# A four-layer graph network on one core: a reordered setup, and one-input maxima for the first batch

## The chip, the core and the metric

The kernel runs on one core of one Trainium2 chip. Time is device time of one execution in microseconds; lower is better. The engines are TensorE (PE, with its weight loads PEld), VectorE (DVE), ScalarE (ACT), GpSimd (POOL) and SyncE (SP); "ACTq" and "SPq" are DMAs that ScalarE's and SyncE's instruction streams issue.

## The reference, cut to what matters

Eight graphs (batches) of 2048 nodes with 256 features, one adjacency matrix of 0 and 1 each. Four layers, each a layer norm, a relu and a graph layer added to x:

```python
# layer 0 (adj_preln)
h = jnp.maximum(_layernorm(x), 0.0)
scores = jnp.where(adj != 0, -jnp.arange(N), -inf)
vals, idx = jax.lax.top_k(scores, 25)          # the first 25 neighbours of each node
feats = h[idx]                                  # gather 25 rows of 256, missing ones -inf
agg = feats.max(axis=2)                         # maximum over the 25 rows
x = x + relu(concat([h, agg]) @ W + b)
# layers 1 and 3: attention over the graph; layer 2: mean over neighbours
```

## The kernel before, in words

Nodes are cut into tiles of 128, 16 per batch (`NT`), 128 in all. Layer 0 of one tile is a *slot* of 16 *parts*. Its front (`slot_front`, tile T+2) loads the adjacency rows (ScalarE's queue, L653), casts them (L648), transposes them on TensorE (L812), packs them into 256 words, copies the keys (L643), and lets VectorE search the first 25 neighbours (L1018 to L1111). Then GpSimd issues 25 indirect gathers of 128 rows of 1 KB each from the table `htab` in HBM into one of two buffers `gath[:, par]` (L587). A gather needs the indices, the whole table of its batch (`h_dma`) and the buffer, free once tile T-2 is reduced (`reduced`). Its back (`slot_back`, tile T) waits for the gathers, takes the maximum on VectorE by halving (L1120 and L1136), transposes it together with h (L837), multiplies by W (L843) and adds to x (L1142), which goes to `x1d`. `pre` normalizes the next batch's rows into the table.

The program (`program`) is: `setup`, `first_h` (the table of batch 0), the fronts of tiles 0 and 1, and then a loop `b = -1` of 8 times 2 slots with layer 0 of batch 0 alone; in its last two slots the gathers of tiles 16 and 17, batch 1's first, begin. Then comes `body` for each batch: layers 1 to 3 with the slots of the next batch's layer 0 between their steps. The order of the instructions on each engine is written out by hand in that way; engines meet at semaphores.

In setup, SP loads x in four blocks (L482, two semaphores, so the third waits for the first), then eleven constants and weights (L498, one semaphore `w_ld`), and writes 2 MB of zeros to the table's second half. Some of the weights are staged in gather buffer 0. VectorE waits for all of `w_ld`, splits the bias into three bf16 parts, folds the attention vectors into w1 and w3 (L1050, L1052), and only then takes the row statistics (L1063, L1007). ScalarE makes h0 (L613), SP stores it (L510), then copies the bias parts (L516). TensorE waits for these copies before tile 0's front. A reduction of another kind, for the attention spread, is at L1181.

Of the kernel before, what the change touches and what calls it, by code (L numbers as in the profile page):

```python
# [37 lines left out]
ALU = mybir.AluOpType  # L38
# [66 lines left out]
def gnn_kernel(nc, x, adj, w0, b0, w1, a1s, a1d, w2m, w2u, b2, w3, a3, const, out):  # L105
    ctx = ExitStack()
    with ctx:
# [92 lines left out]
        EDGES = {1: 4, 3: 8}  # L200
        ring = {p: edge_f.rearrange("p (a c) -> p a c", a=EDGES[p]) for p in EDGES}
        hT = [edge_f[:, 512 * i:512 * i + 512].rearrange("p (t k r) -> p t k r", t=2, k=2) for i in range(2)]
        res = [edge_f[:, 1024 + 512 * i:1536 + 512 * i].rearrange("p (t c) -> p t c", t=2) for i in range(2)]
# [30 lines left out]
        zero_st, zero_set = sem("zero_st"), sem("zero_set")  # L234
        x0_ld, ln0_ok, h0_ok = [sem("x0_ld0"), sem("x0_ld1")], sem("ln0_ok"), sem("h0_ok")
        chain = sem("chain")
# [172 lines left out]
        class Part:  # L409

            def setup(self): pass
            def first_h(self): pass
            def pre(self, u, n, part): pass
            def slot_front(self, T, par, n, part): pass
            def slot_back(self, T, par, n, part, front): pass
            def prep_start(self, p, b): pass
# [14 lines left out]
            def slot(self, b, sh, par, part, front, k):  # L431
# [4 lines left out]

                known = isinstance(sh, int)
                enters = not known or front(2 * sh + par)
                next_enters = not known or front(2 * sh + par + 1)
                Tf, Tb, n = front_tile(b, sh, par), back_tile(b, sh, par), half(b, sh)  # L440
                if part == 0:
                    self.slot_back(Tb, par, n, part, enters)
                if enters:
# [3 lines left out]
                if part != 0:  # L447
                    self.slot_back(Tb, par, n, part, enters)
                if next_enters:
# [23 lines left out]
        def _(sp):  # L473
            class Do(Part):
                def setup(self):
                    sp.sem_inc(u_stored.sem, u_stored.credit)
                    for credit in (x1_dma, xr_ld[0], xr_ld[1]):
                        sp.sem_inc(credit, 16)
                    for g in range(NQ):
                        if g > 1:  # L480
                            sp.wait_ge(x0_ld[g % 2], 16)
                        sp.dma_start(xr[:, BLK * g:BLK * g + BLK, :], x_r[:, BLK * g:BLK * g + BLK, :]).then_inc(x0_ld[g % 2], 16)  # L482
                    kp = "(k p) n -> p k n"
                    tmp = gath[:, 0, :, :]
                    loads = [
                        (cst[:, :], const), (w0_s[:, :, :], w0.rearrange(kp, p=P)),
                        (w1_s[:, :, 0:C], w1.rearrange(kp, p=P)),
                        (w2_s[:, :, 0:C], w2m.rearrange(kp, p=P)), (w2_s[:, :, C:2 * C], w2u.rearrange(kp, p=P)),
                        (tmp[:, 0:2, :], w3.rearrange(kp, p=P)),
                        (tmp[:, 2, :], a1s.rearrange("h f -> (h f)").partition_broadcast(P)),  # L490
                        (tmp[:, 3, :], a1d.rearrange("h f -> (h f)").partition_broadcast(P)),
                        (tmp[:, 4:6, :], a3.rearrange("a (k c) -> (a k) c", k=2).partition_broadcast(P)),
                        (hb_f[0:1, 0:C], b0.rearrange("(a c) -> a c", a=1)),
# [25 lines left out]

# [9 lines left out]

                def slot_back(self, T, par, n, part, front):  # L530
                    if part == 0:
# [63 lines left out]
        def _(act):  # L595
            class Do(Part):
                def setup(self):
                    for c in (a_cast, a_evac, a_copied, a_relu, cat_ev, h_ok[1], h_ok[2], h_ok[3], hT_ok[1], hT_ok[2], hT_ok[3], ev_ok[1], ev_ok[3], wB_ok[1], wB_ok[3], yT_ok, c_cast):
                        act.sem_inc(c.sem, c.credit)
                    act.sem_inc(a_relu.sem, NT)  # L600
                    act.wait_ge(w_ld, 16 * N_LOADS)
                    act.activation(ident_bf[:, :], ident, ACT.Copy).then_inc(w_cast, 1)
# [3 lines left out]
                    act.activation(one_bf, one[P // 2:P // 2 + 1, :].to_broadcast([1, P]), ACT.Copy).then_inc(w_cast, 1)  # L606
                    act.wait_ge(w_tr, 1)
                    act.activation(w3_s[:, :, 0:C], psH[:, :].rearrange("p (k o) -> p k o", k=2), ACT.Copy).then_inc(w_ev, 1)

                def first_h(self):  # L610
                    act.wait_ge(ln0_ok, 1)
                    for t in range(NT):
                        ins = act.activation(h0[:, t, :], xr[:, t, :], ACT.Relu, bias=nm[:, t:t + 1], scale=rs[:, t:t + 1])  # L613
                        if t % BLK == BLK - 1:
                            ins.then_inc(h0_ok, 1)

                def pre(self, u, n, part):
# [42 lines left out]

                def slot_back(self, T, par, n, part, front):
                    if part == 9:
# [127 lines left out]
        def _(pe):  # L790
            class Do(Part):
                def setup(self):
                    for c in (a_used, a_pack, cat_tr, o_done, tp_ok[1], tp_ok[2], tp_ok[3], dn_ok[1], dn_ok[2], dn_ok[3], mm_ok[1], mm_ok[3], c_mm):
                        pe.sem_inc(c.sem, c.credit)
                    pe.wait_ge(w_ld, 16 * N_LOADS)
                    for dk in range(2):
                        for ok in range(2):
                            ins = pe.transpose(psH[:, dk * C + ok * P:dk * C + ok * P + P], gath[:, 0, ok, dk * P:dk * P + P], ident)
                    ins.then_inc(w_tr, 1)
                    pe.wait_ge(w_cast, 5)  # L800
                    pe.wait_ge(w_done, 1)

                def first_h(self):
                    pe.wait_ge(bias_ld, 16 * 6)
# [25 lines left out]

                def slot_back(self, T, par, n, part, front):
                    if part == 7:
# [133 lines left out]
        def _(dve):  # L966
# [57 lines left out]
            class Do(Part):  # L1024
                def setup(self):
                    for c in (a_key, reduced, x1_done, ev_ok[2], edge_ok[1], edge_ok[3], y_ok, x3_ok, x2_ok):
                        dve.sem_inc(c.sem, c.credit)
                    dve.memset(gath[:, 1, 0:NT, :], 0.0).then_inc(zero_set, 1)
                    dve.sem_inc(a_ln.sem, NT)
                    dve.wait_ge(w_ld, 16 * N_LOADS)  # L1030
                    steps.of(dve.tensor_copy(bit_u[:, :], cst[:, C_BIT:C_BIT + WORD]))
                    steps.of(dve.tensor_scalar(hb_f[0:1, 0:C], hb_f[0:1, 0:C], -1.0, None, ALU.add))
# [12 lines left out]
                    dve.sem_inc(bias_cut, 1)  # L1045
                    scratch = cat[:, 0:C]
                    dve.wait_ge(w_ev, 1)
                    for w, k, at, a, H in [(w1_s, k, C, 2, HEADS) for k in range(2)] + [(w1_s, k, C + HEADS, 3, HEADS) for k in range(2)] \
                            + [(w3_s, k, C, 4, 1) for k in range(2)] + [(w3_s, k, C + 1, 5, 1) for k in range(2)]:
                        steps.of(dve.tensor_tensor(scratch, w[:, k, 0:C], gath[:, 0, a, :], ALU.mult))  # L1050
                        steps.wait()
# [5 lines left out]

                def first_h(self):

                    for g in range(NQ):  # L1060
                        dve.wait_ge(x0_ld[g % 2], 16 * (g // 2) + 16)
                        for t in range(BLK * g, BLK * g + BLK):
# [54 lines left out]

                def slot_back(self, T, par, n, part, front):
# [169 lines left out]

N_LOADS = 11
_INS = ["x", "adj", "L0_gnn_W", "L0_gnn_b", "L1_gnn_W", "L1_gnn_a_src", "L1_gnn_a_dst", "L2_gnn_W_msg", "L2_gnn_W_upd",  # L1290
# [16 lines left out]
```

## Time and profile before

| what | value |
|---|---|
| median of 3 runs | 6603.51 us (6597.78 to 6605.72) |
| the profiled execution, own time | 6600.81 us |
| its span in the profile | 6599.0 us |
| busy: TensorE, VectorE, GpSimd, ScalarE | 5100.0, 4633.6, 3467.5, 2099.5 us |
| GpSimd gathers (L587) | 3200, 1084 ns mean |
| halvings (L1120) | 768, 1180 ns mean |
| first gather starts | 73.50 us |
| first attention matmul (L926) starts | 706.55 us |

The time is that of a whole execution, the span what the profile covers of one. A line number in the profile is a line of the kernel. "Busy" leaves out waiting. Shares over the whole span mix the stretch before 700 us with the eight bodies behind it, so the views by window are the ones to read for an edit to the start.

### The profile page before, as it was taken

To read this page: it belongs to the slowest core of one execution; us is meant where nothing else is said; L and a number is where in the kernel's file an instruction comes from. 1 tells how busy PE (TensorE), PEld (TensorE's weight loads), DVE (VectorE), ACT (ScalarE), POOL (GpSimd) and SP (SyncE) were. 2 spreads that over 40 slices of the span, in tenths; PEclk is the share of its full clock that TensorE was granted. 3 is DMA by queue.
4 is the path that set the end of the run, shared out by engine and by line. 5 is a ranking of instruction groups with operands and counts; after the bars stand their busy time and mean duration, and the time that the engine had idled before them with its cause. 6 is when DMAs were issued, how large, how long until landed. Compare 5 with 4: busy or idle time off the path is not lost.

```text
span 6599.0 us, 85899 instructions
## 1 busy us (share of the span) xinstructions
PE 5100.0 (77%) x23860; PEld 3069.2 (47%) x23860; DVE 4633.6 (70%) x9945; ACT 2099.5 (32%) x4103; POOL 3467.5 (53%) x3204
## 2 busy tenths in 40 slices
PE   1222887789878897688877898778976888878998
PEld 1112335563356434573355633664345733555357
DVE  4555786778766787677867787667876778665833
ACT  2222324431343314423244313433144232432131
POOL 4777426773377615774267733776157732771000
PEclk8555998889888898899988898888988999889999
DMA  4544218551284415742185512844157421851040
GB/s 151 157 147 152 74 52 235 171 160 50 78 254 145 130 37 163 216 149 80 51 235 171 161 50 81 253 146 128 37 165 214 152 67 52 237 152 51 0 128 13
DMA packets 660530, 848.85 MB, mean 129 GB/s; under 512 B 80356, under 2 KB 491752, under 8 KB 659944
## 3 DMA queue, kind: packets, MB, share of 16 engines
q0 software_dynamic: 153600, 419.64, 21.6%
q10 hardware_dynamic: 344064, 268.50, 13.9%
q1 hardware_dynamic: 162408, 155.53, 7.3%
q8 instruction: 175, 2.87, 0.2%
q14 instruction: 283, 2.32, 0.1%
HBM read 774.13 MB, written 69.21 MB: 128 GB/s over the span
## 4 chain that ended last, share of the span: by engine, by line
PE 46%; DVE 21%; DMA 12%; issue 8%; POOL 7%; ACT 3%; ACTq 2%; DVEq 1%; SPq 0%; POOLq 0%
PE acc L926 23%; PE acc L930 10%; POOL gath L587 7%; DVE gath L1120 7%; PE acc L874 4%; DMA col_i<-in_adj 4%; DMA hb<-in_adj 3%; DVE edge L1215 3%; DMA gath<-htab,idx 3%; DVE top L1018 2%; DVE key L1021 2%; PE psH L843 2%; PE psB L893 1%; PE acc L958 1%; PE acc L960 1%
## 5 line engine op out<-in xcount | busy, mean ns | idle before, releaser
L587 POOL DMA_INDIRECT gath<-htab,idx x3200 | 3467.3, 1084 | 2511.3 <-issue 2308.1
L1215 DVE SCALAR_TENSOR_TENSOR edge<-region,gg,adjT 128x1024 f32<-128x1024 f32 (+1 forms) x1536 | 1638.7, 1106 | 465.0 <-ACT region L719 231.9
L926 PE MATMUL acc<-edge,region 128*65 128x512 f32 x4096 | 1835.2, 601 | 59.0 <-DVE edge L1215 38.6
L1120 DVE TENSOR_TENSOR gath<-gath 128x1536 f32<-128x1536 f32 (+2 forms) x768 | 896.5, 1180 | 465.9 <-DMA gath<-htab,idx 405.9
L930 PE MATMUL acc<-region,edge 128*128 128x257 f32 x4096 | 999.2, 402 | 141.3 <-DVE xr L1254 90.3
L926 PEld LDWEIGHTS acc<-edge,region 128*65 128x65 f32 x4096 | 553.8, 139 | 1148.6 <-issue 1018.7
L930 PEld LDWEIGHTS acc<-region,edge 128*128 128x128 f32 x4096 | 806.8, 201 | 281.6 <-issue 102.6
L874 PE MATMUL acc<-w_s,edge 128*128 128x512 f32 (+2 forms) x1536 | 583.6, 525 | 0.0
L1018 DVE MAX8 top<-key 128x8 f32<-128x256 f32 (+1 forms) x1024 | 408.1, 399 | 82.2 <-DVE key L1021 36.8
L837 PE MATMUL psH<-cst,cat 128*128 128x128 f32 x512 | 99.0, 326 | 417.4 <-issue 402.0
L627 ACT ACTIVATE adjT_b<-psT 128x1024 bf16<-128x1024 bf16 x256 | 262.3, 1025 | 495.0 <-PE psT L812 482.1
L958 PE MATMUL acc<-region,col_b 128*128 128x257 bf16 x1024 | 295.1, 288 | 148.6 <-ACT col_b L774 88.5
L874 PEld LDWEIGHTS acc<-w_s,edge 128*128 128x128 f32 x1536 | 329.3, 226 | 127.4 <-issue 76.4
L719 ACT ACTIVATE region<-psB 128x512 f32<-128x512 f32 x160 | 95.5, 597 | 869.5 <-PE psB L893 820.1
L759 ACT ACTIVATE col_b<-col_b 128x256 f32<-128x256 f32 x96 | 40.0, 417 | 1024.0 <-DVE col_b L1226 1024.0
L648 ACT ACTIVATE adj_b<-adj_i 128x512 bf16<-128x512 int32 x512 | 313.6, 626 | 99.4 <-DMA adj_i<-in_adj 90.5
L812 PE MATMUL psT<-ident_bf,adj_b 128*128 128x128 bf16 x2048 | 200.2, 251 | 174.5 <-ACT adjT L630 127.5
L843 PE MATMUL psH<-w_s,catT 128*128 128x256 f32 x1024 | 332.2, 480 | 0.0
L958 PE MATMUL acc<-region,edge 128*128 128x257 bf16 x1024 | 283.2, 277 | 43.2 <-ACT edge L774 42.0
L960 PE MATMUL acc<-region,col_b 128*128 128x256 bf16 x1024 | 295.8, 289 | 0.0
L959 PE MATMUL acc<-region,col_b 128*128 128x256 bf16 x1024 | 294.4, 288 | 0.0
L1021 DVE MATCH_REPLACE8 key<-top,key 128x256 f32<-128x256 f32 (+1 forms) x768 | 291.5, 380 | 0.0
(129 smaller groups left out, 5642.3 us busy)
## 6 DMA issues: line engine op xcount, KB each, us to landing
adj_i<-in_adj ACTq DMA_DIRECT2D x512, 256.0 KB, 4.2
hb<-in_adj ACTq DMA_DIRECT2D x256, 256.0 KB
col_i<-in_adj ACTq DMA_DIRECT2D x256, 256.0 KB
gath<-htab,idx POOLq DMA_INDIRECT x3200
cat<-htab SPq DMA_DIRECT2D x128, 128.0 KB
x<-in_x SPq DMA_DIRECT2D x128, 128.0 KB
x1d<-x SPq DMA_DIRECT2D x128, 128.0 KB
xr<-x1d SPq DMA_DIRECT2D x32, 512.0 KB, 4.6
```

The costliest lines, as they stand in the source:

```text
L587: pool.indirect_dma_start(out=gath[:, par, s, :], out_offset=None, in_=htab, in_offset=bass.IndirectOffsetOnAxis(ap=idx[:, par, s:s + 1], ...
L648: act.activation(adj_b[:, k % 2, :], adj_i[:, k % 2, :], ACT.Copy).then_inc(a_cast.sem, 1)
L843: ins = pe.matmul(o_mm, catT[:, k, :], w0_s[:, k, :], start=False, stop=(k == 3))
L874: ins = pe.matmul(bank[:, 0:width], hT[n % 2][:, i, c, :], w[:, c, :], start=(c == 0), stop=(c == 1 and p != 2), skip_group_check=True)
L926: ins = pe.matmul(acc[0:F + 1, 2 * h + half, :], V[1][:, J, (F + 1) * head:(F + 1) * (head + 1)], here[:, 512 * half:512 * half + 512], st ...
L930: ins = pe.matmul(acc[:, k, 0:C + 1], here[:, P * k:P * k + P], V[3][:, J, :], start=(J == 0), stop=(J == NT - 1), skip_group_check=True)
L958: pe.matmul(acc[:, k, 0:C + 1], w, split[:, t, 2 * C:3 * C + 1], start=(t == 0), stop=False, skip_group_check=True)
L960: ins = pe.matmul(acc[:, k, 0:C], w, split[:, t, C:2 * C], start=False, stop=(t == NT - 1), skip_group_check=True)
L1018: steps.of(dve.max(top[:, 8 * r:8 * r + 8], values))
L1021: steps.of(dve.match_replace(values, top[:, 8 * r:8 * r + 8], values, 0.0))
L1120: steps.of(dve.tensor_tensor(gath[:, par, a:a + n, :], gath[:, par, a:a + n, :], gath[:, par, b:b + n, :], ALU.max))
L1215: dve.scalar_tensor_tensor(ring[p][:, n % EDGES[p], :], wB_of[p][:, h, :], gg[:, J, head:head + 1], adjT[:, J, bass.ds(((b + (p - 1)) % 2) ...
```

## The change

Five edits, all in what runs before the first body:

1. The constants are loaded first, with a semaphore of their own (`cst_ld`), and each block of x has its own semaphore. ScalarE's small casts wait for the constants alone.
2. The order of the program becomes: `setup`, tile 0's first adjacency loads (`ahead`), `first_stats` (the statistics of x), tile 0's front with tile 1's first loads and casts, `first_h` (h0 and its store), `weights` (all weight and bias work), tile 1's front, `ready` (where TensorE waits for weights and bias).
3. The credit on `h_dma` that lets gathers begin is given before SP's bias copies.
4. Staged weights and the scratch row lie in the edge buffer instead of the gather buffer and `cat`.
5. In the loop `b = -1` (the 16 tiles of batch 0) the maximum over the 25 rows is taken by four `tensor_reduce` of 64 features each, with one input, instead of six `tensor_tensor` halvings and a last maximum. Tiles of other batches keep the halvings.

```diff
+                    sp.dma_start(cst[:, :], const).then_inc(cst_ld, 16)
                     for g in range(NQ):
-                        if g > 1:
-                            sp.wait_ge(x0_ld[g % 2], 16)
-                        sp.dma_start(xr[...], x_r[...]).then_inc(x0_ld[g % 2], 16)
+                        sp.dma_start(xr[...], x_r[...]).then_inc(x0_ld[g], 16)
...
             do.setup()
-            do.first_h()
             for part in range(PARTS):
                 do.ahead(0, part)
+            do.first_stats()
             for T in range(LAG):
                 for part in range(PARTS):
                     do.slot_front(T, T, 0, part)
                     do.ahead(T + 1, part)
+                if T == 0:
+                    do.first_h()
+                    do.weights()
+            do.ready()
...
                     sp.wait_ge(h_dma, 16 * NQ)
+                    sp.sem_inc(h_dma, 16 * (NT + 1 - NQ))
+
+                def weights(self):
                     sp.wait_ge(bias_cut, 1)
                     for layer, row in ((0, 0), (2, P // 4)):
                         for s in range(3):
                             sp.dma_start(bias[row + s:row + s + 1, 0:C], bias_part(row, s)).then_inc(bias_ld, 16)
-
-                    sp.sem_inc(h_dma, 16 * (NT + 1 - NQ))
...
-                    act.wait_ge(w_ld, 16 * N_LOADS)
+                    act.wait_ge(cst_ld, 16)
...
+                    if alone and part < 4:
+                        if part == 0:
+                            dve.wait_ge(cat_tr.sem, cat_tr.free(T, 1))
+                        c0, c1 = part * C // 4, (part + 1) * C // 4
+                        ins = dve.tensor_reduce(cat[:, C + c0:C + c1], gath[:, par, :, c0:c1].rearrange("p s c -> p c s"), AX, ALU.max)
+                        if part == 3:
+                            ins.then_inc(reduced.sem, 1)
+                        return
```

## Rows read from the trace of the kernel before

**Rows 1.** The page, part 4: the chain that ended last, by engine.

```profile
PE 46%; DVE 21%; DMA 12%; issue 8%; POOL 7%; ACT 3%; ACTq 2%; DVEq 1%; SPq 0%; POOLq 0%
```

**Rows 2.** Windows: length, busy PE PEld DVE ACT POOL, PEclk, DMA, GB/s.

```profile
200.00:400.00 200.00, 46.52 (x276) 32.24 (x276) 111.18 (x295) 46.95 (x70) 154.30 (x151) 0.54 0.52 158
...
700.00:800.00 100.00, 96.10 (x282) 34.75 (x283) 77.58 (x85) 29.33 (x88) 35.21 (x29) 0.95 0.18 54
```

**Rows 3.** Waits of 75 to 600 us: us in total, times, longest.

```profile
DVE gath L1120 <- DMA gath<-htab,idx: 203.6, 15, 22.5
```

**Rows 4.** Waits of 604 to 706 us.

```profile
DVE gath L1120 <- DMA gath<-htab,idx: 23.2, 3, 14.7
```

**Rows 5.** Timeline of 0 to 75 us: start, length, engine, line, what.

```profile
1.01 5.60 SPq L482 DMA_DIRECT2D xr<-in_x  x4
...
18.93 0.31 ACT L602 ACTIVATE ident_bf<-cst 128x128 bf16<-128x128 f32 x1 [15.49 <-DMA hb<-in_L_gnn_bias]
...
30.22 5.33 DVE L1063 BATCH_NORM_STATS2 st<-xr 128x6 f32<-128x256 f32 x16 [0.33 <-DVEq L986]
...
39.30 0.17 DVE L1007 SCALAR_TENSOR_TENSOR nm<-mv,rs 128x16 f32<-128x16 f32 x1
39.51 2.57 ACT L613 ACTIVATE region<-xr,nm,rs 128x256 f32<-128x256 f32 x5 [18.80 <-DVE nm L1007]
...
42.47 5.00 ACT L613 ACTIVATE region<-xr,nm,rs 128x256 f32<-128x256 f32 x10
...
51.16 3.78 SPq L516 DMA_DIRECT2D bias<-hb  x6
...
56.24 1.01 PE L812 MATMUL psT<-ident_bf,adj_b 128*128 128x128 bf16 x8 [36.17 <-issue]
...
59.63 0.63 ACT L648 ACTIVATE adj_b<-adj_i 128x512 bf16<-128x512 int32 x1
...
62.48 0.34 ACTq L653 DMA_DIRECT2D adj_i<-in_adj  x1
62.78 0.39 ACT L643 ACTIVATE cst<-psO 128x256 f32<-128x256 f32 x1
...
66.70 0.63 ACT L648 ACTIVATE adj_b<-adj_i 128x512 bf16<-128x512 int32 x1 [0.42 <-DMA adj_i<-in_adj]
...
72.21 0.24 DVE L1111 TENSOR_SCALAR idx<-top,cst 128x25 uint32<-128x25 f32 x1
...
73.50 1.08 POOL L587 DMA_INDIRECT gath<-htab,idx  x1 [73.04 <-issue]
```

**Rows 6.** Windows of the setup.

```profile
24.00:28.00 4.00, 0.00 (x0) 0.00 (x0) 3.73 (x9) 0.00 (x0) 0.00 (x0) 1.00 0.00 0
```

**Rows 7.** Windows of the gathers alone: length, GpSimd busy, PEclk, DMA, GB/s.

```profile
73.40:104.70 31.30, 23.89 (x25) 1.00 0.50 151
...
139.40:172.60 33.20, 25.65 (x25) 0.55 0.54 158
```

**Rows 8.** Timeline of 304 to 329 us, one tile's halvings and index search.

```profile
306.18 7.47 DVE L1120 TENSOR_TENSOR gath<-gath 128x1536 f32<-128x1536 f32 x6 [11.62 <-DMA gath<-htab,idx]
...
309.06 1.59 POOL L587 DMA_INDIRECT gath<-htab,idx  x1 [0.30 <-issue]
...
312.85 0.95 POOL L587 DMA_INDIRECT gath<-htab,idx  x1 [0.30 <-issue]
313.77 0.43 DVE L1136 TENSOR_TENSOR cat<-gath 128x256 f32<-128x256 f32 x1
...
327.18 0.44 DVE L1111 TENSOR_SCALAR idx<-top,cst 128x25 uint32<-128x25 f32 x1 [0.16 <-DVE top L1018]
```

**Rows 9.** Source lines L1181 and L1052: ns min/median/max, first and last start.

```profile
L1181 DVE TENSOR_REDUCE dmx<-sd x16: 179/224/267, 696.6 to 6468.3; 128x4 f32<-128x64 f32 x8, 128x1 f32<-128x16 f32 x8
...
L1052 DVE TENSOR_REDUCE w_s<-cat x8: 419/420/420, 23.1 to 29.5; 128x4 f32<-128x256 f32 x4, 128x1 f32<-128x256 f32 x4
```

**Rows 10.** Chain in order of time, 0 to 130 us: tile 0's last gather.

```profile
103.79 2.70 DMA gath<-htab,idx
```

More of the change, by code:

```diff
@@ L234, in gnn_kernel @@
         zero_st, zero_set = sem("zero_st"), sem("zero_set")
-        x0_ld, ln0_ok, h0_ok = [sem("x0_ld0"), sem("x0_ld1")], sem("ln0_ok"), sem("h0_ok")
+        x0_ld, ln0_ok, h0_ok, cst_ld = [sem(f"x0_ld{g}") for g in range(NQ)], sem("ln0_ok"), sem("h0_ok"), sem("cst_ld")
         chain = sem("chain")
@@ L411, in setup, with first_stats, weights, ready @@
             def setup(self): pass
+            def first_stats(self): pass
             def first_h(self): pass
+            def weights(self): pass
+            def ready(self): pass
             def pre(self, u, n, part): pass
             def slot_front(self, T, par, n, part): pass
-            def slot_back(self, T, par, n, part, front): pass
+            def slot_back(self, T, par, n, part, front, alone): pass
             def prep_start(self, p, b): pass
@@ L437, in slot @@
                 known = isinstance(sh, int)
+                alone = isinstance(b, int) and b < 0
                 enters = not known or front(2 * sh + par)
@@ L441, in slot @@
                 if part == 0:
-                    self.slot_back(Tb, par, n, part, enters)
+                    self.slot_back(Tb, par, n, part, enters, alone)
                 if enters:
@@ L447, in slot @@
                 if part != 0:
-                    self.slot_back(Tb, par, n, part, enters)
+                    self.slot_back(Tb, par, n, part, enters, alone)
                 if next_enters:
@@ L528, in pre, with slot_back @@
                             sp.dma_start(htab[bass.ds(table_row(u + i), P), :], xa[:, i, :]).then_inc(h_dma, 16)
-                def slot_back(self, T, par, n, part, front):
+                def slot_back(self, T, par, n, part, front, alone):
                     if part == 0:
@@ L615, in first_h, with weights @@
                             ins.then_inc(h0_ok, 1)
+                def weights(self):
+                    act.wait_ge(w_tr, 1)
+                    act.activation(w3_s[:, :, 0:C], psH[:, :].rearrange("p (k o) -> p k o", k=2), ACT.Copy).then_inc(w_ev, 1)
                 def pre(self, u, n, part):
@@ L659, in ahead, with slot_back @@
                         self.cast(T, part - 14)
-                def slot_back(self, T, par, n, part, front):
+                def slot_back(self, T, par, n, part, front, alone):
                     if part == 9:
@@ L794, in setup, with weights @@
                         pe.sem_inc(c.sem, c.credit)
+                    pe.wait_ge(w_cast, 5)
+                def weights(self):
                     pe.wait_ge(w_ld, 16 * N_LOADS)
@@ L829, in slot_front, with slot_back @@
                         pack((3, 7).index(part))
-                def slot_back(self, T, par, n, part, front):
+                def slot_back(self, T, par, n, part, front, alone):
                     if part == 7:
@@ L1029, in setup, with weights @@
                     dve.sem_inc(a_ln.sem, NT)
+                    dve.wait_ge(cst_ld, 16)
+                    steps.of(dve.tensor_copy(bit_u[:, :], cst[:, C_BIT:C_BIT + WORD]))
+                def weights(self):
                     dve.wait_ge(w_ld, 16 * N_LOADS)
-                    steps.of(dve.tensor_copy(bit_u[:, :], cst[:, C_BIT:C_BIT + WORD]))
                     steps.of(dve.tensor_scalar(hb_f[0:1, 0:C], hb_f[0:1, 0:C], -1.0, None, ALU.add))
@@ L1045, in setup @@
                     dve.sem_inc(bias_cut, 1)
-                    scratch = cat[:, 0:C]
+                    scratch = edge_f[:, 6 * C:7 * C]
                     dve.wait_ge(w_ev, 1)
@@ L1049, in setup @@
                             + [(w3_s, k, C, 4, 1) for k in range(2)] + [(w3_s, k, C + 1, 5, 1) for k in range(2)]:
-                        steps.of(dve.tensor_tensor(scratch, w[:, k, 0:C], gath[:, 0, a, :], ALU.mult))
+                        steps.of(dve.tensor_tensor(scratch, w[:, k, 0:C], w_tmp[:, a, :], ALU.mult))
                         steps.wait()
@@ L1056, in setup, with first_stats @@
                     dve.wait_ge(w_done, 1)
-                def first_h(self):
+                def first_stats(self):
                     for g in range(NQ):
-                        dve.wait_ge(x0_ld[g % 2], 16 * (g // 2) + 16)
+                        dve.wait_ge(x0_ld[g], 16)
                         for t in range(BLK * g, BLK * g + BLK):
@@ L1116, in slot_front, with slot_back @@
                         steps.end()
-                def slot_back(self, T, par, n, part, front):
+                def slot_back(self, T, par, n, part, front, alone):
                     def halve(a, b, n):
@@ L1123, in slot_back @@
                         dve.wait_ge(gathered[par], 16 * S * n + 16 * S)
+                    if alone and part < 4:
[6 more added lines that the diff above has]
+                        return
+                    if part == 0:
                         halve(0, 12, 6)
@@ L1286, in _ @@
             program(dve, Do())
-N_LOADS = 11
+N_LOADS = 10
 _INS = ["x", "adj", "L0_gnn_W", "L0_gnn_b", "L1_gnn_W", "L1_gnn_a_src", "L1_gnn_a_dst", "L2_gnn_W_msg", "L2_gnn_W_upd",
```

21 lines of the change are left out of this document (9 added, 12 removed).

## The prediction

> **What bounds the kernel now.** I read the page first, its chain above all. 46% of the chain that ended last is TensorE and only 7% is GpSimd [rows 1], so most of the run is not touched by an edit to the start. Then the windows by stage [rows 2]: between 200 and 400 us, inside the 16 tiles of the first batch's layer 0, TensorE is busy 46.5 of 200 us while GpSimd is busy 154.3; between 700 and 800 us it is the other way round (96.1 of 100 for TensorE). So the run has a head, about 0 to 700 us, in which nothing but setup and layer 0 of batch 0 runs, and a body in which each batch's layer 0 lies beside attention work. The waits of the head say who is last there: from 75 to 600 us VectorE waits 15 times, 203.6 us in all, for gathers to land, once per tile [rows 3]; from 604 to 706 us, across the start of the body, it still waits 23.2 us for tiles 15, 16 and 17 [rows 4]. GpSimd's gathers are therefore the clock of the head: when the first one starts, and how long 25 of them take.
>
> The timeline of the first 75 us [rows 5] shows why the first gather starts at 73.50. Weights land at 18.9 (first cast), VectorE folds the bias and the attention vectors until 30.2, only then takes the 16 row statistics (30.22 to 39.30 + 0.17), ScalarE makes h0 (39.51 to 47.47), the store and its landing hold SP until 51.16, SP issues six bias copies, TensorE starts on tile 0 at 56.24 only when they have landed, and the index search ends at 72.2. One long serial chain, with the DMA engines idle in it from 24 to 28 us [rows 6].
>
> **The change, part one: setup.** Nothing is computed less; work leaves the chain. Removed from it: 30.22 - 18.93 = 11.3 us of weight work on VectorE, and the bias copies ahead of TensorE, 56.24 - 51.16 = 5.1 us. Besides, tile 0's front now runs before h0 is made. The new chain, step by step:
> - The constants are SP's first load, issued at 1.0 as x is now. A 256 KB adjacency load of the head, issued from 62.48 on as one of two, is cast at 66.70 [rows 5], so 4.2 us: the constants are there at 5.2, and five small ScalarE casts of 0.3 us or less end at 6.4.
> - ScalarE issues tile 0's first two loads at 6.4. Alone they would take 4.2 us; x, the weights and the 2 MB of zeros are in flight, so I take 6. Two casts of 0.63: 13.7, say 14. The second pair, issued then, lands after about 5 more: the last cast starts at 19.5.
> - From the last cast to the copy of the keys is 62.78 - 59.63 = 3.15 us [rows 5]: 22.7. The index search, 72.21 - 62.78 = 9.4 and 0.2 for its last instruction, ends at 32.3.
> - ScalarE has tile 1's two casts ahead of h0 in its queue: 67.33 - 62.78 = 4.55 us, to 27.2. The statistics (9.3 us, x there by 15 at the latest) end at 24.4, hidden under this. The 16 h0 instructions, 7.96 us, end at 35.2; the last store lands 51.16 - 47.47 = 3.7 later, at 38.9. The gather needs table and indices; the table is last. Gather issue after its last releaser: 73.50 - 72.45 = 1.05. First gather at 39.9, that is 33.6 us earlier.
>
> Bounds: with every load at 4.2 us it comes to 36.8 (a gain of 36.7). If tile 0's second pair lands only when all loads have drained (now over by 24 [rows 6]; 0.75 MB of adjacency on top of 6.3 MB of x, weights and zeros, so 25), the key copy is at 28.2 and the gather at 45.4 (a gain of 28.1). What waits behind the moved work: SP waits for the zeros until some 25 us, before the first h0 block is due at 29. VectorE's weight work waits for ScalarE's copy of w3, now behind h0 (35.8), and ends near 43; the six bias copies go out from 38.9 and land near 44. TensorE needs both only before the first loop slot, whose first data (tile 0 gathered) comes at 73. Tile 1's indices: ScalarE starts on it at 36, and the same 3.15 + 9.6 us behind its second pair of loads give about 55; they are needed 31 us after the first gather, at 71. The cover is 16 us. Without it the delay would be one for one. The aliases (weights staged in the edge buffer) cost nothing: edge is idle until the body.
>
> **Part two: the maxima.** In each tile of the first batch the halvings are six instructions and a last one, 306.18 to 313.65 and 0.43 more, 7.9 us, two SBUF inputs each. While they run, three gathers take 1.59 us instead of 0.95 [rows 8]; in between stays 0.30. By windows: 25 gathers with no halving beside them take 31.3 us of time and 23.89 busy, a tile with halvings 33.2 and 25.65 [rows 7]. The replacement is four reductions with one input, 25 x 64 = 1600 elements each, at a stride of 1 KB. If they leave GpSimd alone, each tile saves 3 x (1.59 - 0.95) = 1.92 us; they lie beside the gathers of tiles 1 to 16, so 16 x 1.92 = 30.7 us. For "leave alone" the evidence is the rest of the same rows: VectorE works from 313.8 to 327.6 on statistics and searches, nearly all with one SBUF input or short, and the gathers beside it are back at 0.95 from 312.85 on. No reduction of this size is in the trace, so the bounds are 0 (still 1.59) and 30.7; I take 30.7. The Trainium skill ("SBUF — State Buffer", Who interferes with whom) says that tensor_reduce never contends with GpSimd on trn2, which would give 30.7, and infers that tensor_tensor takes only the read side of the shared ports, which descriptor generation does not need; by that inference the 1.59 is not the halvings' doing. Here the row disagrees with the inference: the long gathers sit exactly beside the halvings.
>
> How long a reduction is: the contiguous one of 256 elements takes 0.42 us; the strided one goes from 0.179 us for 16 elements to 0.267 for 64, 1.8 ns an element [rows 9]. So 1.8 us each at one nanosecond and a bit per element, or 3.1 us at 1.8: R = 7.2 to 12.3 us a tile against 7.9. It is nearest in kind to the strided row, and it does not matter: from landing to indices VectorE needs 21.4 us, 13.5 without the halvings; the last gather is issued 2.7 us before it lands [rows 10], so the indices of the tile after next must be there 31.3 - 2.5 = 28.8 us after a landing. R is hidden up to 15.3 us.
>
> **Sum.** 33.6 + 30.7 = 64.3 us off the head. The body follows: x of tile 15, tiles 16 and 17 and so the first attention come from the same gathers [rows 4], and nothing in it is changed. Span 6599.0 - 64.3 = 6534.7; the execution's own time 6600.81 becomes 6536.5; the median of before is 2.7 above that execution, so 6539.
>
> **Rivals.**
> - *The gathers stay long.* Either the reductions hold GpSimd up too, or the 1.59 has another cause. Against it: the single-input work beside gathers at 0.95. For it: no long reduction has been seen beside a gather, and the inference quoted above. Only setup gains: 6603.5 - 33.6 = 6570.
> - *The strided reduction is slow* and VectorE becomes late with the indices: beyond R = 15.3 every tile's pitch grows by (R - 15.3)/2, since an index is used two tiles later. The whole gain of 64.3 over 16 tiles, 4.0 a tile, is gone at R = 23.3, that is 5.8 us an instruction or 3.6 ns an element, twice the dearest strided row. At 4 ns (6.55 each, R = 26.2) the pitch grows by 5.4: 87 - 64 = 23 slower, 6627. Between 15.3 and 23.3 it lies between 6539 and 6603. The Trainium skill ("Advanced Engine Details and Errata", Memory Cachelines) warns of a penalty when each access goes to another 16-byte line; it gives no size, and the 1.8 ns row has such a stride already.
> - *The setup loads collide:* tile 0's adjacency, the weights and the zeros share the DMA engines; the bound above, 6603.5 - 28.1 - 30.7 = 6545. I count this into the forecast's own range.
>
> **How the numbers follow.** Forecast 0.80 (own range 6532 to 6550: from 36.7 + 30.7 + 4 for noise and later matters, to 28.1 + 30.7 with 5 on top), gathers stay long 0.12, reduction slow enough to matter 0.08: half of it short of 6603, half slower. About 0.7 lies in the own range, so the range must take in 6570 as well: 6530 to 6573. A measurement of this kernel can tell 0.2%, 13 us, from no change. Faster: 0.80 + 0.12 + 0.03 = 0.95; same 0.02; slower 0.03.
>
> **What would show it.** First gather at 37 to 45 us; in ScalarE's order tile 0's key copy, tile 1's casts, then h0, and the store of h0 as the gather's last releaser. All gathers of tiles 1 to 16 at 0.95 and a pitch of 31.3, against 33.2. Reductions of 1.8 to 3.1 us. First attention matmul at about 642 instead of 706.55, and from there the two traces equal. Wrong if gathers beside a reduction are above 1 us, if VectorE's wait for gathers vanishes, or if the first gather follows the index search instead of the store.

## The result, and the profile after

The changed kernel takes 6531.31 us in the median of 5 runs (6526.52 to 6541.70), the kernel before 6601.72 (6595.58 to 6605.72). The ratio is 0.9897, 95% interval 0.9883 to 0.9910: 59 to 77 us less. Forecast were 6539 and 64 us less. The profiled execution is the slowest of its five, 6541.70 us with a span of 6539.8; its span is 59.2 us shorter than before's. Six of the runs below stand beside a kernel before that took 7958 to 7975 us, where it took 6596 to 6602 beside the others; what differs was not found, and they are called the 7960 us runs.

The order of work in the setup came out as forecast. The timeline of the changed kernel, to be held against [rows 5]:

```profile
3.92 0.31 ACT L610 ACTIVATE ident_bf<-cst 128x128 bf16<-128x128 f32 x1 [0.49 <-DMA cst<-in_const]
...
10.28 0.63 ACT L658 ACTIVATE adj_b<-adj_i 128x512 bf16<-128x512 int32 x1 [5.20 <-DMA adj_i<-in_adj]
...
17.67 0.17 DVE L1019 SCALAR_TENSOR_TENSOR nm<-mv,rs 128x16 f32<-128x16 f32 x1
...
21.36 0.63 ACT L658 ACTIVATE adj_b<-adj_i 128x512 bf16<-128x512 int32 x1 [2.30 <-DMA adj_i<-in_adj]
...
24.52 0.39 ACT L653 ACTIVATE cst<-psO 128x256 f32<-128x256 f32 x1
...
27.43 1.33 ACT L658 ACTIVATE adj_b<-adj_i 128x512 bf16<-128x512 int32 x2 [2.52 <-DMA adj_i<-in_adj]
...
28.67 3.04 ACT L619 ACTIVATE region<-xr,nm,rs 128x256 f32<-128x256 f32 x6
...
31.62 5.01 ACT L619 ACTIVATE region<-xr,nm,rs 128x256 f32<-128x256 f32 x10
...
33.95 0.24 DVE L1126 TENSOR_SCALAR idx<-top,cst 128x25 uint32<-128x25 f32 x1
...
40.49 3.79 SPq L526 DMA_DIRECT2D bias<-hb  x6
...
41.41 1.08 POOL L595 DMA_INDIRECT gath<-htab,idx  x1 [40.95 <-SPq L520]
```

The statistics are ready at 17.8 and wait, ScalarE copies tile 0's keys at 24.5, casts tile 1 and only then makes h0 (28.7 to 36.6). The indices are there at 34.2; the gather starts at 41.41, released by SP's credit behind the stored table. The bias copies leave beside it instead of ahead of tile 0.

The gathers by windows, against [rows 7], and one tile, against [rows 8]. In the first fence the columns are length, GpSimd busy (instructions), PEclk, DMA share and GB/s:

```profile
41.30:72.60 31.30, 23.88 (x25) 1.00 0.56 167
104.20:135.50 31.30, 23.66 (x25) 0.55 0.53 159
```

```profile
265.71 11.02 DVE L1143 TENSOR_REDUCE cat<-gath 128x64 f32<-128x1600 f32 x4 [6.89 <-DMA gath<-htab,idx]
265.88 0.95 POOL L595 DMA_INDIRECT gath<-htab,idx  x1 [0.30 <-issue]
...
274.63 0.94 POOL L595 DMA_INDIRECT gath<-htab,idx  x1 [0.30 <-issue]
...
289.80 0.24 DVE L1126 TENSOR_SCALAR idx<-top,cst 128x25 uint32<-128x25 f32 x1 [0.16 <-DVE top L1030]
```

A tile with its reductions beside the gathers now takes 31.3 us, as one without. All gathers of tiles 1 to 16 are at about 0.95, and none is above 1.14. The four reductions take 11.0 us where the halvings took 7.9, and VectorE still waits for the gathers afterwards: the waits of 50 to 545 us, against [rows 3], and the source lines of the new reductions, of the first step of each attention spread, against [rows 9], and of the attention matmuls:

```profile
DVE cat L1143 <- DMA gath<-htab,idx: 139.7, 16, 19.7
```

```profile
L1143 DVE TENSOR_REDUCE cat<-gath x64: 2808/2814/2827, 74.6 to 552.6; 128x64 f32<-128x1600 f32 x64
...
L1205 DVE TENSOR_REDUCE dmx<-sd x16: 179/223/267, 633.8 to 6409.1; 128x4 f32<-128x64 f32 x8, 128x1 f32<-128x16 f32 x8
...
L938 PE MATMUL acc<-edge,region x4096: 591/592/1112, 643.7 to 6231.7; 128*65 128x512 f32 x196
```

The first attention matmul starts at 643.7, where about 642 was forecast and before had 706.55. The row of L1205 is the ruler for what follows. L1205 (L1181 before) runs first at the end of the first body's prep, 633.8 against 696.6, and last in the last batch, 6409.1 against 6468.3. So 62.8 us come out of the head; from there to the last spread the two kernels take 5775.3 and 5771.7 us. One row of the page's chain, against [rows 1]; the share of GpSimd falls from 7% to 5%:

```profile
PE 49%; DVE 19%; DMA 13%; issue 8%; POOL 5%; ACT 3%; ACTq 2%; DVEq 1%; SPq 0%; POOLq 0%
```

### The profile page after: what moved, and what is told of

It reads as the page before. It is cut to its first block, busy times and chain, and to the rows that moved or that the text cites. A ratio compares the mean times of both kernels' runs of the same rounds, so it can differ in the third digit from the quotient of the medians.

```text
span 6539.8 us, 85786 instructions
## 1 busy us (share of the span) xinstructions
PE 5101.5 (78%) x23860; PEld 3069.3 (47%) x23860; DVE 4692.1 (72%) x9897; ACT 2100.4 (32%) x4103; POOL 3433.4 (53%) x3204
## 4 chain that ended last, share of the span: by engine, by line
PE 49%; DVE 19%; DMA 13%; issue 8%; POOL 5%; ACT 3%; ACTq 2%; DVEq 1%; SPq 0%; POOLq 0%
PE acc L938 23%; PE acc L942 12%; POOL gath L595 5%; DMA hb<-in_adj 5%; PE acc L886 4%; DVE gath L1135 4%; DMA col_i<-in_adj 3%; DVE edge L1239 3%; PE psH L855 2%; DVE top L1030 2%; DVE cat L1143 2%; DMA gath<-htab,idx 2%; DVE key L1033 2%; PE psB L905 1%; PE acc L970 1%
## 5 line engine op out<-in xcount | busy, mean ns | idle before, releaser
L1135 DVE TENSOR_TENSOR gath<-gath 128x1536 f32<-128x1536 f32 (+2 forms) x672 | 784.1, 1180 | 232.1 <-DMA gath<-htab,idx 179.3
```

## The experiments

Each run has its own neighbour runs of the kernel before; ratios are against these. The 7960 us runs are setup_only once, maxima_only and reductions_twice twice each, and pairs_long_output. Their times are not compared with the others', and only what their rows show by themselves is used of them.

### Taking the two parts apart

Setup alone: the changed kernel with the old halvings.

```diff
-                    if alone and part < 4:
+                    if False and part < 4:
```

> The reordered setup with the old halvings in every tile. Theory (two independent parts, added): first gather at 41.4 us as in the changed kernel, pitch of the first batch's tiles 33.2 us, three gathers of 1.59 us a tile, 16 x 1.92 = 30.7 us slower than the changed kernel: about 6565 to 6570. Rival (the gain of the maxima comes from elsewhere, or the long gathers are not the halvings' doing): gathers at 0.95 and a time near 6535.

This is a 7960 us run: 7948.05 us against 7975.10, ratio 0.9971 (0.9933 to 1.0009). One of its twelve executions took 17924 us; it is not in the ratio, and its cause is not known. The kernel was run again.

> The reordered setup with the old halvings in every tile, once more, beside a kernel before that runs at its 6600 us. Theory: first gather at 41 to 46 us, pitch 33.2, three gathers of 1.59 us a tile beside the halvings, 30.7 us slower than the changed kernel: about 6565. Rival (the long gathers cost nothing): near 6535.

6573.71 us against 6596.34, ratio 0.9965 (0.9951 to 0.9979): 14 to 32 us less. That is 9 us above the expected 6565; the head by itself is 30 us shorter than before's (table below). The first gather is at 43.66. Its gathers by windows:

```profile
108.40:141.70 33.30, 25.69 (x25) 0.78 0.53 158
141.70:174.90 33.20, 25.61 (x25) 0.55 0.53 158
```

So the pitch stays 33.2, with three gathers above 1.2 us in each of tiles 1 to 17. The rival (time near 6535) is out.

Maxima alone: the old setup with the reductions.

```diff
+                    if alone and part < 4:
+                        if part == 0:
+                            dve.wait_ge(cat_tr.sem, cat_tr.free(T, 1))
+                        c0, c1 = part * C // 4, (part + 1) * C // 4
+                        ins = dve.tensor_reduce(cat[:, C + c0:C + c1], gath[:, par, :, c0:c1].rearrange("p s c -> p c s"), AX, ALU.max)
```

> The old setup with the one-input reductions in the first batch's tiles. Theory: first gather at 73.5 us, pitch 31.3, no gather above 1.1 us beside a reduction, 30.7 us faster than before: about 6571. Rival (the reductions pay only with the new setup, or something else bounds the pitch): pitch 33.2 and a time within 5 us of before, 6602.

> The old setup with the one-input reductions, once more, beside a kernel before that runs at its 6600 us. Theory: first gather at 73.5 us, pitch 31.3, no gather above 1.1 us beside a reduction, 30.7 us faster than before: about 6570. Rival (VectorE's longer work, 11.0 us instead of 7.9, or something else sets the pitch): pitch 33.2, time within 5 us of before.

Both are 7960 us runs: 8003.49 against 7975.10 us, ratio 1.0032 (1.0001 to 1.0064), and 8027.87 against 7957.64, ratio 1.0104 (1.0042 to 1.0166). There the pitch is not set by the gathers. In the first half of the 16 tiles it is 38.6 us and VectorE's search itself pauses, as a row of the second run shows (before the 0.43 us instruction VectorE sat idle 2.25 us for nothing that the profile places on this core). In the second half the pitch is 31.4 and 51.2 us by turns, and before each long one VectorE waits some 28 us for ScalarE to copy the keys. The last row below sums that wait for 75 to 600 us (total, times, longest).

```profile
L587 POOL DMA_INDIRECT gath<-htab,idx x418: 942/946/1088, 74.4 to 719.9; - x140
```

```profile
244.44 0.43 DVE L1018 MAX8 top<-key 128x8 f32<-128x256 f32 x1 [2.25 <-remote]
```

```profile
DVE key L1088 <- ACT cst L643: 59.3, 3, 28.7
```

What the run shows is the first row: with the old setup too, none of the 418 gathers up to 720 us, those beside the reductions among them, is above 1.09 us. What the maxima alone are worth in time at 6600 us was not measured; it follows only as the difference between the changed kernel and setup_only. In these two runs the maxima did not make the kernel faster; why both ratios are above 1 was not traced.

The changed kernel once more, as a neighbour for the runs below.

> The changed kernel unchanged, as the neighbour of the next three on the same chip: ratio 0.990 to before as measured, 6525 to 6540. If the difference between the profiled execution (59 us less span than before) and the medians (70 us less) is chance between executions, the gain comes out between 60 and 72 us here too, and the head's 63 us is the same in the profile.

6537.47 us against 6599.05, ratio 0.9907 (0.9894 to 0.9921): 52 to 70 us less. The first gather is at 46.08, not 41.41, and the last spread at 6400.2, earlier than in the first profile. The rows tell what moved:

```profile
22.58 0.63 ACT L658 ACTIVATE adj_b<-adj_i 128x512 bf16<-128x512 int32 x1 [7.24 <-DMA adj_i<-in_adj]
26.02 0.63 ACT L658 ACTIVATE adj_b<-adj_i 128x512 bf16<-128x512 int32 x1 [1.90 <-DMA adj_i<-in_adj]
29.17 0.39 ACT L653 ACTIVATE cst<-psO 128x256 f32<-128x256 f32 x1
...
46.08 1.08 POOL L595 DMA_INDIRECT gath<-htab,idx  x1 [45.62 <-SPq L520]
```

From the last cast on, everything is as in the first profile (3.15 us to the key copy, 16.9 more to the gather). The last of tile 0's adjacency pieces landed 4.7 us later.

With eight profiles the head can be read as a sum. "Spread" is the first start of the L1181/L1205 reduction:

| kernel | first gather | first spread | between | first to last spread |
|---|---|---|---|---|
| before | 73.5 | 696.6 | 623.1 | 5771.7 |
| setup_only (b) | 43.7 | 666.1 | 622.4 | 5774.9 |
| changed | 41.4 | 633.8 | 592.4 | 5775.3 |
| changed, again | 46.1 | 638.6 | 592.5 | 5761.6 |
| h0_before_casts | 40.8 | 633.3 | 592.5 | 5759.2 |
| weights_first | 52.0 | 642.6 | 590.6 | 5764.4 |
| weights_after_fronts | 33.8 | 624.8 | 591.0 | 5771.6 |
| reductions_everywhere | 40.5 | 634.2 | 593.7 | 5904.0 |

The maxima are the step from 623 to 592: 30.6 us between before and the changed kernel. The setup is the first column. The last column has nothing of either in it, but for the last row, and its first seven values scatter by 16 us. The setup of the last row is that of the changed kernel, so its 40.5 is a fourth profile of one setup, beside 41.4, 46.1 and 43.7.

### What holds the gathers up

The changed kernel with reductions over pairs of rows: one input each, but a long output like a halving's.

```diff
+                        def pairs(to, fr):
+                            steps.of(dve.tensor_reduce(to, fr.rearrange("p (s two) c -> p s c two", two=2), AX, ALU.max))
...
+                            pairs(rg[:, 0:6, :], gath[:, par, 0:12, :])
+                            pairs(rg[:, 6:12, :], gath[:, par, 12:24, :])
+                            pairs(rg[:, 12:18, :], rg[:, 0:12, :])
```

> The changed kernel with the maximum of the first batch's tiles in three reductions over pairs of rows (one input of 3072 elements, a long output of 1536 as the halvings have) and four short two-input steps. Tells what holds the gathers up. If it is two SBUF inputs: gathers beside the pair reductions at 0.95 us, only beside the step of 768 perhaps one above. If it is the long output stream to SBUF or the length of the instruction: several gathers of 1.5 us or more a tile. Pair reductions at 1.7 ns an element take 5.2 us each, so R near 17.5 and the pitch up by about 1 us; time 6530 to 6560 either way.

This is a 7960 us run (7968.21 us, one execution). The rows of one tile:

```profile
243.84 6.91 DVE L1143 TENSOR_REDUCE region<-gath 128x1536 f32<-128x3072 f32 x2
...
246.32 0.95 POOL L595 DMA_INDIRECT gath<-htab,idx  x1 [0.30 <-issue]
...
250.89 3.39 DVE L1143 TENSOR_REDUCE region<-region 128x1536 f32<-128x3072 f32 x1
...
252.57 0.94 POOL L595 DMA_INDIRECT gath<-htab,idx  x1 [0.30 <-issue]
...
254.31 1.52 DVE L1146 TENSOR_TENSOR region<-region 128x768 f32<-128x768 f32 x2
255.07 1.02 POOL L595 DMA_INDIRECT gath<-htab,idx  x1 [0.30 <-issue]
```

Reductions of 3.39 us with 1536 outputs leave the gathers at 0.95; only in 5 of 16 tiles one gather is above 1.2 us (1.29 at most), and short two-input steps remain there. Of 137 gathers in this trace that lay mostly beside a pair reduction none took over 1.2 us; of 338 that lay mostly beside a halving of 1536 elements in the kernel before, 269 did. So neither the length of the instruction nor its output holds GpSimd up; of what was varied, the second input is left. The expected 5.2 us for a reduction was wrong; see the last section.

One thing was varied with it: a halving reads its 3072 elements in 1.76 us, a pair reduction in 3.39, so the reading is also half as fast. The bodies of the kernel before speak against that as the cause. There L1215 has two SBUF inputs, 1024 elements of 4 bytes and 1024 of 1 byte in 1.28 us, 4.0 bytes a nanosecond and partition; the pair reduction reads 3.6. Beside L1215 gathers do get long:

```profile
702.08 1.28 DVE L1215 SCALAR_TENSOR_TENSOR edge<-region,gg,adjT 128x1024 f32<-128x1024 f32 x1 [2.45 <-ACT region L719]
702.35 1.83 POOL L587 DMA_INDIRECT gath<-htab,idx  x1 [0.30 <-issue]
```

Of the 391 gathers that had L1215 (with 1024 or 512 elements) and nothing else of VectorE's beside them, 109 took over 1.2 us. How long a gather becomes, and why not every one does, was not traced.

### Where a longer reduction would stop being free

The changed kernel with each reduction done twice, the extra one into scratch.

```diff
+                        steps.of(dve.tensor_reduce(region[:, c0:c1], gath[:, par, :, c0:c1].rearrange("p s c -> p c s"), AX, ALU.max))
+                        steps.end()
```

> The changed kernel with each of the four reductions of a tile done twice (the extra one into a scratch row), R = 22.1 us a tile instead of 11.0. Theory A (an index is used two tiles later, so lateness is halved, (R - 15.3) / 2 = 3.4 a tile): 54 us slower than the changed kernel, about 6586. Theory B (VectorE works through 22.1 + 13.1 for the rest of the tile to the indices + about 1 without a pause, pitch 36.2 to 36.6 against 31.3): 80 to 86 us slower, about 6615, and VectorE waits for gathers next to nothing. Theory C (it stays hidden): 6531.

> Each reduction of the changed kernel done twice, R = 22.3 us a tile instead of 11.0, beside a kernel before that runs at its 6600 us. Theory A (lateness of the indices halved, (R - 15.3) / 2 = 3.5 a tile): 56 us slower than the changed kernel, about 6590. Theory B (VectorE without a pause, pitch 22.3 + 13.1 + about 1 = 36.4 to 36.7): 82 to 87 us slower, about 6618, GpSimd idle 5 us before each tile's first gather and VectorE's waits for gathers near nothing. Theory C (hidden): 6535.

Both are 7960 us runs: 7906.89 against 7975.10 us, ratio 0.9913 (0.9878 to 0.9947), and 7904.20 against 7957.64, ratio 0.9955 (0.9915 to 0.9994). The times that the theories gave can't be tested there. Their order of events can, in the second run:

```profile
208.39 0.24 DVE L1126 TENSOR_SCALAR idx<-top,cst 128x25 uint32<-128x25 f32 x1 [0.16 <-DVE top L1030]
...
209.37 2.81 DVE L1143 TENSOR_REDUCE region<-gath 128x64 f32<-128x1600 f32 x1
209.43 0.95 POOL L595 DMA_INDIRECT gath<-htab,idx  x1 [11.82 <-issue]
...
251.56 0.24 DVE L1126 TENSOR_SCALAR idx<-top,cst 128x25 uint32<-128x25 f32 x1 [0.16 <-DVE top L1030]
```

GpSimd sits idle 11.8 us before the tile's first gather, which starts 0.8 us after the indices are ready, and VectorE goes from the indices straight into the next reduction. After the first tile it waits for no gather. That is theory B's picture, VectorE as the clock. The pitch is 42.7 to 43.2 us in the first half of the tiles and 36.8 to 37.6 in the second; VectorE's pauses of over 0.45 us, which the 6600 us profiles do not have, add up to about 6 and 4 us a tile in them. Without these it would be about 37 and 33.

Neither theory had two halves, but the changed kernel's own profile has them. Its windows over four tiles of each half (length, VectorE busy, PEclk, DMA share, GB/s), in which VectorE waits 25.2 and 40.4 us for gathers:

```profile
135.60:260.90 125.30, 90.38 (x196) 0.54 0.57 168
417.40:542.90 125.50, 77.91 (x128) 0.54 0.50 150
```

Without those waits VectorE needs 25.0 us a tile in the first half and 21.3 in the second, that is 14.0 and 10.3 besides the reductions: in the first eight slots it also takes the statistics of batch 1's rows. So an estimate for R = 22.6 is 36.6 and 32.9 a tile against 31.3, some 55 us over 16 tiles. Theory B's 82 to 87 took the first half for all; theory A's 56 would be near for another reason. The time itself was not measured.

### Reductions in every batch

```diff
-                    if alone and part < 4:
+                    if part < 4:
```

> The reductions in every batch instead of the first alone. Theory A (in the bodies GpSimd is not last and VectorE is near its limit): 112 tiles get 3.1 us more VectorE work each, 347 us in all; at a third to a half of it exposed 100 to 170 us slower than the changed kernel, 6630 to 6700. Theory B (what counts is that gathers are not held up in the bodies either): up to 2 us a tile faster, 6531 or below.

6668.38 us against 6599.05, ratio 1.0108 (1.0092 to 1.0123): 131 us slower than the changed kernel beside it. Windows over one body, first of the changed kernel and then of this one (busy of PE, PEld, DVE, ACT, POOL; then PEclk, DMA share, GB/s):

```profile
1000.00:1771.00 771.00, 638.38 (x2983) 383.61 (x2982) 579.10 (x1253) 261.47 (x512) 436.95 (x400) 0.89 0.46 137
```

```profile
1000.00:1771.00 771.00, 634.61 (x2946) 383.68 (x2947) 622.26 (x1178) 257.80 (x506) 386.38 (x392) 0.88 0.45 133
```

The stretch is one body of the changed kernel; of this one, whose bodies are longer, it holds 392 of 400 gathers. VectorE is busy 43 us more in it, GpSimd 51 us less: a gather is busy 0.99 us on average instead of 1.09, so it is the gathers that gain and the kernel that loses. Over the whole trace, of 941 gathers that had a reduction and nothing else of VectorE's beside them none took over 1.2 us. The head is the same, 40.5 and 634.2. Theory A holds: 112 tiles x 3.1 us = 347 us more VectorE work, of which 131, 38%, shows. In the bodies the gathers have slack and VectorE has little.

### The setup, step by step

h0 ahead of tile 1's first casts in ScalarE's queue:

```diff
                 for part in range(PARTS):
                     do.slot_front(T, T, 0, part)
                     do.ahead(T + 1, part)
+                    if T == 0 and part == 8:
+                        do.first_h()
                 if T == 0:
-                    do.first_h()
                     do.weights()
```

> The changed kernel with h0 made as soon as tile 0's keys are copied, ahead of tile 1's first casts in ScalarE's queue. Theory (the table is the last releaser of the first gather): h0 starts at 24.9 instead of 28.7 and the first gather at 37.7 instead of 41.4; 3.7 us faster, 6527, below what the time can tell, to be read in the profile. Rival (the index search, ending at 34.2, or the zeros and h0's store colliding in the DMA engines take over): first gather at 41 still.

6529.72 us against 6599.05, ratio 0.9897 (0.9881 to 0.9912); the changed kernel beside it took 6537.47, and the two intervals overlap. The rows:

```profile
27.88 0.39 ACT L654 ACTIVATE cst<-psO 128x256 f32<-128x256 f32 x1
28.45 7.97 ACT L620 ACTIVATE region<-xr,nm,rs 128x256 f32<-128x256 f32 x16 [0.17 <-issue]
...
40.81 1.08 POOL L596 DMA_INDIRECT gath<-htab,idx  x1 [40.35 <-SPq L521]
```

From the key copy to the gather it is 12.9 us instead of 16.9, so the 4 us are there. The first gather is nevertheless at 40.8: the key copy was at 27.9 here, against 24.5 and 29.2 in the two profiles of the changed kernel. The forecast of 37.7 for the gather failed on the landing of the second pair: the last cast was at 24.7.

The weight work put back ahead of tile 0:

```diff
+            do.weights()
             do.first_stats()
...
                 if T == 0:
                     do.first_h()
-                    do.weights()
```

> The changed kernel with the weight and bias work put back ahead of the statistics and of tile 0. Theory (11.3 us of the 32.1 come from taking the weights off the chain, the rest from not waiting for the bias copies and from running tile 0's front before h0): statistics end near 39.5, h0 at 47.5, first gather near 52.3, 10.9 us slower than the changed kernel: 6542. Rival (the weights lie beside loads that are late anyway): first gather within 3 us of 41.4.

6549.79 us against 6599.05, ratio 0.9927 (0.9914 to 0.9941), 12.3 us more than the changed kernel beside it. The rows:

```profile
38.95 2.56 ACT L619 ACTIVATE region<-xr,nm,rs 128x256 f32<-128x256 f32 x5 [5.98 <-DVE nm L1019]
...
51.95 1.08 POOL L595 DMA_INDIRECT gath<-htab,idx  x1 [51.49 <-SPq L520]
```

First gather at 51.95, 5.9 to 10.5 us behind the two profiles of the changed kernel; h0 starts at 38.95, when the statistics end. So the weights' place is worth 6 to 10 us of the setup's 27 to 32. The rest is 73.50 - 51.95 = 21.5 us: what came behind the stored table in the kernel before, the bias copies (51.16 to 56.24) and tile 0's front (56.24 to the gather at 73.50), 22.3 us in all [rows 5], now lies beside h0 or behind the gather. These two were not taken apart by a run.

Weights and zeros out of the way of the second pair:

```diff
+                    sp.wait_ge(a_cast.sem, a_cast.ready(3))
...
-                    sp.wait_ge(zero_st, 48)
...
                     sp.wait_ge(h_dma, 16 * NQ)
+                    sp.wait_ge(zero_st, 48)
                     sp.sem_inc(h_dma, 16 * (NT + 1 - NQ))

                 def weights(self):
+                    for to, fr in loads:
+                        sp.dma_start(to, fr).then_inc(w_ld, 16)
                     sp.wait_ge(bias_cut, 1)
```

Here SP issues the zeros behind the four casts of tile 0, and the weights behind h0's store; h0 comes after tile 0's key copy as above, `weights` after tile 1's front.

> h0 as in the run h0_before_casts, and besides SP issues the zeros only when tile 0's four adjacency pieces are cast, and the weights only after h0 is stored; the weight work comes after tile 1's front. Theory (the second adjacency pair lands late because weights and zeros share the DMA engines with it: 5 to 10 us from issue to landing, against 3 to 4 alone): last cast of tile 0 near 16.7 us, key copy near 20, first gather near 33 instead of 41 to 46; 8 to 13 us faster than the changed kernel, 6520 to 6527. Rival (something else holds the second pair, or the zeros now collide with h0's store): first gather at 38 or later, no faster than the run with h0 before the casts. And if the weights are now too late, tile 1's gather starts more than 31.6 us after tile 0's.

6526.05 us against 6596.34, ratio 0.9888 (0.9873 to 0.9904), the best of all. The timeline:

```profile
15.39 0.63 ACT L658 ACTIVATE adj_b<-adj_i 128x512 bf16<-128x512 int32 x1 [0.67 <-DMA adj_i<-in_adj]
16.83 0.62 ACT L658 ACTIVATE adj_b<-adj_i 128x512 bf16<-128x512 int32 x1
...
19.98 0.39 ACT L653 ACTIVATE cst<-psO 128x256 f32<-128x256 f32 x1
...
21.37 7.97 ACT L619 ACTIVATE region<-xr,nm,rs 128x256 f32<-128x256 f32 x16 [1.00 <-issue]
...
33.77 1.08 POOL L595 DMA_INDIRECT gath<-htab,idx  x1 [33.31 <-SPq L505]
```

Windows of 12 to 16 us, first here, then in the changed kernel's second profile:

```profile
12.00:16.00 4.00, 1.92 (x17) 1.09 (x17) 3.28 (x24) 2.26 (x4) 0.00 (x0) 1.00 0.40 131
```

```profile
12.00:16.00 4.00, 1.80 (x17) 1.08 (x17) 2.63 (x21) 2.11 (x3) 0.00 (x0) 1.00 1.10 353
```

With the DMA engines at 131 GB/s instead of 353 the last cast is at 16.8 instead of 21.4 or 26.0, and the gather at 33.8, as forecast. Some 4 us of that are h0's place, as in the run before; whether the weights or the zeros held the second pair was not taken apart. Tile 1's gathers start 32.1 us after tile 0's (31.6 in the changed kernel), so the later weights cost 0.5 us at most. The head is 9 to 14 us shorter than the changed kernel's by the profiles. The times differ by 5 to 11 us, not measured side by side, and the intervals of the ratios overlap: that it beats the kernel before is measured, that it beats the changed kernel is shown by the profile only.

## Why the prediction was right

- **The bound.** The head is set by the start of the gathers and their pitch: shown by the table, where the stretch between first gather and first spread is 622.4 to 623.1 us with halvings and 590.6 to 593.7 with reductions, while the first gather moves from 33.8 to 73.5.
- **Setup, 33.6 us forecast, 32.1, 27.4, 29.8 (setup_only) and 33.0 (reductions_everywhere) measured** from the first gather. The order of steps was right, each with the releaser named. The term that was sized too small is the landing of tile 0's second pair: last cast forecast at 19.5, measured 21.4, 26.0, 23.6 and 19.5. The forecast had both bounds for it (a gather at 36.8 and at 45.4); the second profile with 46.1 lies just beyond the late one, which counted 0.75 MB for tile 0's four pieces of 256 KB. That the setup came out near 33.6 in two profiles of four is in part luck. The constants were earlier than forecast (3.9 instead of 5.2), tile 1's indices came at 54.9 where 55 was said, the bias copies at 40.5 instead of 38.9.
- **Maxima, 30.7 us forecast, 30.6 measured** between the changed kernel and before (623.1 to 592.4), and 30.0 against setup_only. The times bear it out coarsely: the ratio of setup_only, 0.9965, against 0.9907 and 0.9897 is 38 to 45 us, with some 13 of uncertainty.
- **R, 7.2 to 12.3 us forecast, 11.0 measured,** as the strided row of [rows 9] had it rather than the contiguous one. It stayed hidden: VectorE waits 139.7 us for gathers where it waited 203.6 [rows 3]. But the cover is uneven: the forecast's 13.5 us besides the halvings were read in the first half of the tiles, where it is thin. In tiles 3 to 9 a gather starts only 2.1 to 3.9 us after its indices are there, in tiles 11 to 17 9.1 to 9.6 us.
- **Rivals.** "The gathers stay long" is out. The Trainium skill ("SBUF — State Buffer", Who interferes with whom) infers that tensor_tensor does not stall descriptor generation; for these indirect gathers it does not hold, since beside tensor_tensor they go from 0.95 to 1.59. The same section also says that a VectorE instruction with two SBUF inputs contends with a GpSimd instruction that reads SBUF; these gathers take their indices (`idx`) from there, and the rows fit that. Its rule that on trn2 tensor_reduce never contends agrees with all 64 reductions of the first batch. "The strided reduction is slow" is out at R = 11.0. The price of a longer reduction was reckoned with (R - 15.3) / 2 alone. VectorE's own work, R + 14.0 us a tile in the first half and R + 10.3 in the second, is another limit; an estimate from it gives the break-even near R = 23 as well, so the forecast's 23.3 is right by luck if it is right. No run measured it.
- **The sum.** 64.3 forecast, 62.8 and 58.0 in the heads of the two profiles, 70 and 62 in the medians. The difference between head and median was not traced; the bodies, which the change does not touch, scatter by 16 us from profile to profile, which is enough for it.

## What to carry to other kernels

Where GpSimd's indirect gathers are the clock, count what each long VectorE instruction with two SBUF inputs beside them costs them (here three gathers of 1.59 us instead of 0.95 a tile), and trade it for a one-input form if VectorE has slack there; the same trade in the bodies, where VectorE has little, cost 131 us. Take the slack where it is least, not as an average over the tiles. Before a loop that is paced by one engine, every microsecond of setup counts one for one (here within 3 us): order the first loads by what the first unit of that engine needs, and keep bulk loads out of their way rather than only behind them in one queue.

## What the runs showed that was not expected

- A one-input maximum over 25 rows at a stride of 1 KB takes 2.81 us for 1600 elements, about 1.8 ns an element; a maximum over pairs of rows at the same stride takes 3.39 us for 3072, 1.1 ns. So it is not the stride alone. The cause was not sought.
- The last of tile 0's 256 KB loads, issued between 12.3 and 13.6 us, was cast 7 to 12 us later in five profiles with weights and zeros in flight, the last cast lying at 19.5, 21.4, 23.6, 24.7 and 26.0 us, and 4 us later, at 16.8, without them. Four of the five have the same setup. One profile of a setup is not enough to size it.
- In the 7960 us runs VectorE paused 2 to 3 us before single instructions in the first tiles, and the maxima alone did not make the kernel faster (1.0032 and 1.0104). Whether this goes with the chip is not known: the record gives its numbers 4 and 7 for them, and 0 and 7 for the experiments at 6600 us. A gain that rests on one engine being last need not carry over to where another is; that this is the reason was not shown.
